# A decoder layer with a mixture of experts: the high and low part of the down weights side by side in one 512-column product

## What is computed

```python
logits = h @ router_w.T
probs = softmax(logits)
vals, idx = lax.top_k(probs, 2)
vals = vals / vals.sum(axis=-1, keepdims=True)
combine = zeros((T, E)).at[arange(T)[:, None], idx].add(vals)
def step(acc, per_expert):
    gup, dp, cw = per_expert
    gate, up = jnp.split(h @ gup.T, 2, axis=-1)
    y = silu(gate) * up @ dp.T
    return acc + cw[:, None] * y, None
out, _ = lax.scan(step, zeros_like(h), (gate_up_proj, down_proj, combine.T))
x = layernorm(x + out)
```

## Time and profile before

| | before |
|---|---|
| median of 3 runs | 160.91 us (160.43 to 162.19) |
| span of the profiled execution | 160.5 us |
| PE busy | 146.4 us, 91%, 1158 products |
| PE weight loads busy | 139.7 us, 87% |
| DVE busy | 111.2 us, 69% |
| ACT busy | 86.9 us, 54% |
| POOL busy | 81.0 us, 50% |

### The profile page before, as it was taken

How to read it: one execution, slowest core, us unless ns; L and a number is a source line. 1 busy time by engine, 2 the same in 40 slices (tenths; PEclk the granted TensorE clock), 3 DMA queues, 4 the chain that set the end, 5 groups by cost and what they waited for, 6 DMA issues and landing times.

```text
span 160.5 us, 3397 instructions
## 1 busy us (share of the span) xinstructions
PE 146.4 (91%) x1158; PEld 139.7 (87%) x1158; DVE 111.2 (69%) x385; ACT 86.9 (54%) x187; POOL 81.0 (50%) x131
## 2 busy tenths in 40 slices
PE   6778579987899999999999999999999999999980
PEld 6566457876799998999999999999999999999970
DVE  3999957989888979699827886966735652444252
ACT  6431496489876787735466866355554404335210
POOL 5613499486966468622119564224835213337421
PEclk9999987999999999999999999999999999999998
DMA  3899990000000374000246100017430025620001
GB/s 104 263 383 422 354 325 22 0 0 0 6 0 4 87 150 121 7 0 4 66 154 146 35 0 33 6 30 158 135 111 0 0 55 122 159 62 6 33 0 65
DMA packets 13313, 14.55 MB, mean 91 GB/s; under 512 B 1744, under 2 KB 13040, under 8 KB 13040
## 3 DMA queue, kind: packets, MB, share of 16 engines
q1 hardware_dynamic: 13296, 14.34, 29.7%
HBM read 13.25 MB, written 1.08 MB: 89 GB/s over the span
## 4 chain that ended last, share of the span: by engine, by line
PE 75%; DMA 7%; DVE 6%; ACT 3%; SPq 3%; issue 2%; POOL 1%; POOLq 0%; ACTq 0%
PE ps_gu L351 13%; PE ps_gu L356 13%; PE ps_gu L352 13%; DMA gu_raw<-in_guT 7%; PE ps_out L372 6%; PE ps_out L376 6%; PE ps_out L373 6%; PE ps_ab L385 3%; PE ps_ab L390 2%; PE ps_s L385 2%; ACT gu_hi L775 1%; PE ps_gu L407 1%; PE ps_ab L486 1%; SPq L255 1%; PE ps_tr L322 1%
## 5 line engine op out<-in xcount | busy, mean ns | idle before, releaser
L351 PE MATMUL ps_gu<-x_hi,gu_hi 128*128 128x256 f32 x176 | 46.5, 286 | 0.0
L352 PE MATMUL ps_gu<-x_hi,gu_lo 128*128 128x256 f32 x176 | 45.6, 281 | 0.0
L1185 POOL TENSOR_TENSOR gu_raw<-gu_raw 128x512 f32<-128x512 f32 (+1 forms) x24 | 28.5, 1196 | 22.2 <-DVE gu_raw L1575 14.8
L356 PE MATMUL ps_gu<-x_lo,gu_hi 128*128 128x256 f32 x176 | 35.2, 282 | 0.0
L351 PEld LDWEIGHTS ps_gu<-x_hi,gu_hi 128*128 128x128 f32 x176 | 33.1, 188 | 0.1
L352 PEld LDWEIGHTS ps_gu<-x_hi,gu_lo 128*128 128x128 f32 x176 | 33.2, 188 | 0.0
L356 PEld LDWEIGHTS ps_gu<-x_lo,gu_hi 128*128 128x128 f32 x176 | 27.0, 188 | 0.0
L1581 DVE TENSOR_TENSOR hid_lo<-gu_raw,hid_hi 128x512 fp32r<-128x512 f32 (+1 forms) x24 | 15.0, 636 | 13.8 <-ACT hid_hi L811 13.8
L811 ACT ACTIVATE hid_hi<-gu_raw 128x512 fp32r<-128x512 f32 (+1 forms) x24 | 14.2, 594 | 13.0 <-POOL gu_raw L1185 12.8
L372 PE MATMUL ps_out<-dp_hi,hid_hi 128*128 128x256 f32 x77 | 20.4, 286 | 0.0
L1575 DVE TENSOR_TENSOR gu_raw<-sil,ps_gu 128x512 f32<-128x512 f32 (+1 forms) x24 | 15.2, 636 | 6.8 <-PE ps_gu L356 4.6
(11 more groups left out here) (271 smaller groups left out, 309.0 us busy)
## 6 DMA issues: line engine op xcount, KB each, us to landing
gu_raw<-in_guT SPq DMA_DIRECT2D x1, 2824.0 KB, 12.0
gu_raw<-share_rows SPq DMA_DIRECT2D x16, 128.0 KB, 3.2
dp_raw<-in_dpT SPq DMA_DIRECT2D x1, 1408.0 KB, 15.3
u_feat<-in_xT SPq DMA_DIRECT2D x4, 256.0 KB, 4.1
w_feat<-in_wT SPq DMA_DIRECT2D x4, 256.0 KB, 9.7
out<-u_feat SPq DMA_DIRECT2D x8, 128.0 KB, 2.0
gu_raw<-share_rows SPq DMA_DIRECT2D x8, 112.0 KB, 2.9
gu_raw<-share_rows SPq DMA_DIRECT2D x8, 96.0 KB, 2.9
```

Of the source, the lines that this page charges most:

```text
L351: pe.matmul(dst, gu_hi[:, c, kind, col], x2_hi[:, b % 2, c], start=(c == 0), stop=False)
L352: pe.matmul(dst, gu_lo[:, c, kind, col], x2_hi[:, b % 2, c], start=False, stop=False)
L356: last = pe.matmul(dst, gu_hi[:, c, kind, col], x2_lo[:, b % 2, c], start=False, stop=(c == DC - 1))
L1185: pool.tensor_tensor(hid[:, lo:hi], hid[:, lo:hi], shares[:, lo:hi], ALU.mult).then_inc(hid_ready, 1)
```

## The change

`dp_hi` and `dp_lo` become two halves of one tensor `dp_parts`, so that the 256 high and 256 low weights of a chunk lie next to each other in a partition. `down` issues one product of 512 moving columns where it issued two of 256. The hi*hi sum then gathers in the first half of the bank and the hi*lo sum in the second; the lo*hi products go to the first half as before. `moe_add` has to add both halves: two instructions, the second of which waits for the first.

```diff
-        ps_moe = [[ps_out[:, 0:D]] * TT] * (B - 1) + [[ps_out[:, 0:D], ps_a[:, 0:D]]]
+        ps_moe = [[ps_out[:]] * TT] * (B - 1) + [[ps_out[:], ps_a]]
...
-        dp_hi, dp_lo = sb("dp_hi", [P, HC, D], F32R), sb("dp_lo", [P, HC, D], F32R)
+        dp_parts = sb("dp_parts", [P, HC, 2, D], F32R)
+        dp_hi, dp_lo = dp_parts[:, :, 0], dp_parts[:, :, 1]
...
                 for h in range(lo, hi):
-                    pe.matmul(dst, hid_hi[:, h, tok], dp_hi[:, h], start=(h == 0), stop=False)
-                    pe.matmul(dst, hid_hi[:, h, tok], dp_lo[:, h], start=False, stop=False)
+                    pe.matmul(dst, hid_hi[:, h, tok], dp_parts[:, h].rearrange("p k d -> p (k d)"), start=(h == 0), stop=False)
                 pe.wait_ge(hid_lo_ready, count_of(b, p))
                 for h in range(lo, hi):
-                    last = pe.matmul(dst, hid_lo[:, h, tok], dp_hi[:, h], start=False, stop=(h == HC - 1))
+                    last = pe.matmul(dst[:, 0:D], hid_lo[:, h, tok], dp_hi[:, h], start=False, stop=(h == HC - 1))
...
-                dve.tensor_tensor(s3[:, t], ps_moe[b][t], x2[:, b % 2, t], ALU.add).then_inc(moe_read, 1)
+                then(dve.tensor_tensor(s3[:, t], ps_moe[b][t][:, 0:D], x2[:, b % 2, t], ALU.add))
+                dve.tensor_tensor(s3[:, t], ps_moe[b][t][:, D:2 * D], s3[:, t], ALU.add).then_inc(moe_read, 1)
```

## The result

The changed kernel takes 163.66 us (median of 4 runs, 162.03 to 164.09) against 160.75 for the kernel before beside it (160.43 to 162.19). The ratio on record, of the fast runs of both, is 1.0122, with a 95% interval of 1.0066 to 1.0177; the two medians alone would give 1.018. The forecast was 160.9 with a range up to 161.9.

The account below looks back on a forecast made before the run. The prediction took PE, busy 91% of the span, as the bound, with a chain of small steps at the end. Its terms -0.80 + 0.46 + 0.29 = -0.05 us against 160.91 gave 160.9 us, range 159.9 to 161.9.

Parts of the forecast that it names:

- I take 0.217, near the fp32 row, since the router rows speak for the load: In `down` on PE, one 512-column product was to take 0.217 us against 0.229 a pair, saving 12 ns.
- the columns set the pace: Rival for PE's `down` products: 512 columns cost twice 256, nothing saved, both sum costs stand, 161.7 us; 15%.
- The router rows: Router products of 16 and 8 columns, 0.11 us apart on PE, taken to show that the weight load sets most of the pace.
- PE gives 0.80: Saving on PE from fused `down` products: 0.68 from 57 pairs, plus 0.02 and 0.10 kept at two tight places, 0.80 us.
- The two costs of the second sum: Delays from the added DVE sum at `moe_add(3, 1)` and `moe_add(1, 0)`: +0.46 and +0.29 us.
- +0.46 at the tail: The second sum of `moe_add(3, 1)` stands on the end chain with nothing beside it: +0.46 us.
- +0.29 at `expert_out(3)`: The second sum of `moe_add(1, 0)` delays `moe_norm(1, 0)`, then `unround_both(3)`, for which PE waits: +0.29 us.
- The six hidden sums: The other six `moe_add` second sums were to cost nothing; if all were uncovered, 6 x 0.46 = 2.8 us.
- the last rival: DVE becomes the bound: the six other sums reach PE through `gated` or `hid_lo`, 163.7 us; 8%.
- The named tight places on PE: `x2_transpose(2)`, `expert_out(3)` and `hid_lo(3, 5)`, where PE would wait on other engines and keep only 0.02, nothing and 0.10 us.
- within 1%: Whole kernel: the measured time differs from the kernel before by no more than 1%; 87%.
- the chance of 8% for slower by over 1%: Whole kernel: a time over 162.5 us, expected only if DVE becomes the bound; 8%.

Follow-up runs that it names:

- `after_again`: The changed kernel measured once more, nothing altered: 162.80 us, ratio 1.0032 to the kernel before.
- `after_32_fewer`: The changed kernel without the eight warming products at PE's start, 32 instructions fewer: 163.33 us, ratio 1.0079 to the kernel before.
- `after_third`: The changed kernel measured a third time, nothing altered: 162.58 us, ratio 1.0060 to the kernel before.
- `one_product_one_sum`: The changed kernel with the fused product kept but the second sum dropped, leaving out the hi*lo part: 162.34 us, ratio 1.0002 to the kernel before.
- `adq_first`: The changed kernel with `unround_both(3)` ahead of `moe_norm(1, 0)` in ACT's list: 162.50 us, ratio 1.0024 to the kernel before.
- `two_products_two_sums`: The changed kernel with the fused product split again into two of 256 columns, both sums kept: 162.69 us, ratio 1.0005 to the kernel before.
- `before_64_fewer`: The kernel before without 16 of its warming products, 64 PE instructions fewer: 161.62 us, ratio 0.9966 to the kernel before.
- `before_bf16`: The kernel before with the `down` weights, `hid_hi` and `hid_lo` in bf16: 159.35 us, one run.
- `before_adq_x2`: The kernel before with `unround_both(3)` ahead of `moe_norm(1, 0)` on ACT and `rstd2(3)` ahead of batch 2's share products on POOL: 165.58 us, ratio 1.0225.
- `x2_first`: The changed kernel with `rstd2(3)` ahead of the two share products of batch 2 in POOL's list: 165.07 us, ratio 1.0192 to the kernel before.

## Why the prediction was wrong, step by step

**"I take 0.217, near the fp32 row, since the router rows speak for the load": wrong, and it is the failed step of the sum, the term of -0.80.** A product of 512 fp32r columns costs 0.226 to 0.236. The rival "the columns set the pace" said 0.227 to 0.237 and nothing saved, and that is what came. The router rows were read wrongly. They show that products of few columns, each with a load, follow each other at 0.111 to 0.112 (25 of 28 distances), which is a floor of its own; they don't show that 256 columns would fit under it. Here the two floors nearly coincide (0.111 and 0.113), and taking one away leaves the other. And the row was of another type, plain fp32: its 0.215 is near the bf16 pace (0.216), not that of fp32r.

**"PE gives 0.80": it took some 0.3 instead.** Where the write is in time the stage is +1.01 (`after_again`; 1.02 in `after_32_fewer`; less the stall, 1.05 in the profile of the result and in `after_third`). The sums are 0.72 of it, so the fused stream costs 0.29; `one_product_one_sum` gives 0.29 by itself. Of it 0.21 lies in the pieces of `down` themselves (30.91 against 30.70), some 0.13 of that in the last stretch, where 0.69 stands against 0.68. In some stretches with busy neighbours it gained, 0.71 to 0.69, but in the sum the losses are larger. The other 0.08 I can't place.

**The two costs of the second sum: right.** +0.46 at the tail, measured 0.47; +0.29 at `expert_out(3)`, measured 0.25, and `one_product_one_sum` and `adq_first` show both mechanisms. **The six hidden sums: right for the changed kernel**, no new gap stands behind any of them; but with less room than thought, as the gap of 0.14 in `two_products_two_sums` shows. DVE didn't become the bound (71% busy), so the last rival didn't come about, although the time came out near its 163.7, which is luck.

**The named tight places on PE**: `x2_transpose(2)` and `hid_lo(3, 5)` show no wait of note in the changed kernel, since PE came no earlier.

**The place I didn't name.** This is the second failed step, a term put at nothing without a reason. I had asked of each wait what the second sum or an earlier PE would do to it, and passed over `x2_transpose(3)`, which has over a microsecond of room for either. What used that room up, and 0.5 to 1.15 us more in the fp32r kernels without reordering, was a write that signalled 1.7 to 2.3 us late. The removed instructions were costed by their time on PE; that they are also code, which is fetched by DMA while the kernel runs, was no step of mine. Whether that code is the cause stays open, as said above; the wait itself is 1.15 of the 2.20 us in the profile of the result.

**Range and chances.** The columns' rival gave 161.7; with the fused stream's 0.3 it would have been 162.0, a little outside the range. Between 0.3% and 1.2% slower in three comparisons, "within 1%" was not far off for the typical run, but the chance of 8% for slower by over 1% came from DVE alone and was too small for what I had no mechanism for. No change that keeps the numbers' type was shown to beat the kernel before: the lowest ratio is that of `before_64_fewer`, whose interval holds 1. `before_bf16` is at 159.35, one run and a less exact result.

## What to carry to other kernels

Before fusing products to save weight loads, measure both floors in their own data type; where products of the size at hand already run at the columns' pace, the fusion saves next to nothing, and an extra sum behind it is paid on every chain that has no room for it (here two of eight). When a wait appears that the edit can't explain, follow the chain back to the first piece whose length changed (here a DMA write of 8 KB, 1.3 us in one profile and 3.6 in the other) before blaming the engines in it. And moving one engine's instruction forward helps only if the next engine's list has nothing in front of its user that the move makes late.

## What the hardware showed that I had not expected

- fp32r columns are not as fast as bf16 ones: 512 in 0.226 to 0.236 us against 0.216, 256 in 0.113 to 0.118 against 0.109. In the quiet stretches a product of 512 is 10 ns longer when an `hid_lo` product follows (0.236) than when another product of 512 does (0.226); in bf16 both are 0.216. Why isn't known.
- One packet of a small write can pass 1.1 to 1.5 us behind the other seven, in seven of seven cases just as a fetch of PE's code (16 KB, 0.9 to 1.3 us) ended, and the issue that waits for the write comes 1.7 to 2.3 us late. It was seen only where PE's stream had 8 fetches and not 9; with 256 waits added behind the last product, whose code runs 50 us later, it was absent in two profiles. That isn't enough to call the fetch the cause.
- A gap of 2.20 us on PE was followed by 3.5 us at a mean granted clock of 0.53 (`before_adq_x2`); one of 1.89 in `x2_first` was not (1.00).
